# Lag projections in 32-column strips, normalisation on ScalarE, Gram sums per group, and ternary weights loaded and rounded behind the lag chain, in a two-layer kernel

## What is computed

```python
def _L0_xattn_ref(Q, K, V, Wq, bq, Wout, bout):      # K_TOP = 12, 16 heads of 16
    q, k_, v = ((a @ Wq + bq).transpose(0, 2, 1) for a in (Q, K, V))
    corr = real(ifft(fft(q) * conj(fft(k_)))).mean(axis=(0, 1))
    W_topk, I_topk = top_k(corr, K_TOP);  W_topk = softmax(W_topk)
    R = sum(w * roll(v, -shift) for w, shift in zip(W_topk, I_topk))
    return heads_side_by_side(R) @ Wout + bout
...
def _weight_quant(w):
    scale = 1.0 / clip(mean(abs(w)), 1e-05)
    return clip(round(w * scale), -1.0, 1.0) / scale
...
x = x + _L0_xattn_ref(layernorm(x), ctx, ctx, ...)
x = x + top1_of_8_experts(layernorm(x), ...)
x = x + masked_attention_16_heads(layernorm(x), ctx, ctx, mask, ...)
x = x + bitlinear(silu(bitlinear(layernorm(x), w_gate)) * bitlinear(layernorm(x), w_up), w_down)
```

## Time and profile before

| what | value |
|---|---|
| three runs | 1537.13, 1540.78, 1541.70 us (median 1540.78) |
| the profiled execution's own time | 1551.78 us |
| its span | 1550.0 us, mean granted TensorE clock 0.915 |
| busy: PE, weight loads, DVE, ACT, POOL | 1268.1, 878.3, 1097.4, 958.6, 691.8 us |
| mean DMA rate over the span | 140 GB/s |
| the chain that ended last | PE 47%, DVE 22%, issue 14%, ACT 5%, DMA 4% |

### The profile page before, as it was taken

One profiled execution on the slowest core, in us unless ns is written; L12 is line 12 of the kernel. 1 busy time (PEld: TensorE's weight loads), 2 busy tenths in 40 slices (PEclk: granted clock), 3 DMA queues, 4 the chain that ended last, 5 costly groups with the idle time before them and its releaser, 6 DMA issues.

```text
span 1550.0 us, 29933 instructions
## 1 busy us (share of the span) xinstructions
PE 1268.1 (82%) x9486; PEld 878.3 (57%) x9486; DVE 1097.4 (71%) x3076; ACT 958.6 (62%) x1846; POOL 691.8 (45%) x854
## 2 busy tenths in 40 slices
PE   4962365688899989998999899989998999888875
PEld 4851354456566656665666566656665666555543
DVE  4753342458788878887888788878886777777754
ACT  1220231257777767776777777767766777777774
POOL 2312334235544554456445644565446444444331
PEclk9985586699999989998999999999998999999996
DMA  8772354445445445554544455545444444333200
GB/s 273 228 255 56 99 178 146 142 145 157 142 149 155 152 139 150 152 158 134 151 150 150 151 153 148 154 141 150 142 140 127 132 145 126 120 104 103 76 9 14
DMA packets 169174, 216.84 MB, mean 140 GB/s; under 512 B 19002, under 2 KB 157628, under 8 KB 162492
## 3 DMA queue, kind: packets, MB, share of 16 engines
q1 hardware_dynamic: 162876, 198.15, 41.8%
q0 software_dynamic: 6144, 16.79, 3.2%
HBM read 133.33 MB, written 79.43 MB: 137 GB/s over the span
## 4 chain that ended last, share of the span: by engine, by line
PE 47%; DVE 22%; issue 14%; ACT 5%; DMA 4%; POOL 4%; SPq 3%; DVEq 0%; another core or an unknown queue 0%; POOLq 0%; ACTq 0%
DVE mx L1104 8%; PE mx_pair L1369 5%; PE bank L1330 5%; PE ex_pair L1314 4%; PE bank L1442 4%; PE bank L1340 4%; PE bank L1396 3%; PE mx_pair L1292 3%; PE bank L1390 3%; DVE small L1160 3%; PE mx_pair L1356 3%; PE bank L1450 2%; PE bank L1410 2%; DVE t L1155 2%; DVE bn L899 2%
## 5 line engine op out<-in xcount | busy, mean ns | idle before, releaser
L1104 DVE TENSOR_REDUCE mx<-mx_pair 128x4 f32<-128x1024 f32 x256 | 312.7, 1222 | 60.0 <-PE mx_pair L1369 36.2
L694 POOL TENSOR_TENSOR hid<-hid,t 128x256 f32<-128x256 f32 x256 | 196.3, 771 | 227.4 <-DVE t L1155 226.0
L846 ACT ACTIVATE pt<-ex_pair 128x1024 f32<-128x1024 f32 x256 | 262.1, 1024 | 26.0 <-PE ex_pair L1314 25.8
L1369 PE MATMUL mx_pair<-ks,qs 62*128 62x256 f32 x1024 | 133.3, 336 | 67.8 <-DVE mx L1104 57.8
L1330 PE MATMUL bank<-pt,va 128*32 128x256 f32 x2048 | 169.7, 404 | 2.0 <-ACT ot L852 1.9
L1369 PEld LDWEIGHTS mx_pair<-ks,qs 62*128 62x128 f32 x1024 | 85.6, 196 | 144.0 <-DVE mx L1104 120.1
L871 ACT ACTIVATE hid<-bank 128x256 f32<-128x256 f32 x256 | 98.6, 385 | 109.0 <-PE bank L1340 100.3
L1314 PE MATMUL ex_pair<-qs,ks 64*128 64x256 f32 x1024 | 132.5, 338 | 7.8 <-ACT pt L846 7.7
L1442 PE MATMUL bank<-ew,xst 128*128 x480 | 125.5, 406 | 6.4 <-ACT xst L815 6.2
L1155 DVE SCALAR_TENSOR_TENSOR t<-th,bank 128x256 f32<-128x256 f32 x256 | 106.8, 417 | 33.5 <-ACT th L877 21.2
L661 POOL TENSOR_TENSOR rs<-ve,mhalf 128x2 f32<-128x2 f32 x96 | 68.6, 714 | 132.1 <-DVE ve L905 112.0
(11 more groups left out here) (212 smaller groups left out, 2757.4 us busy)
## 6 DMA issues: line engine op xcount, KB each, us to landing
ks<-ksplit_d SPq DMA_DIRECT2D x192, 128.0 KB
qs<-qsplit_d SPq DMA_DIRECT2D x192, 128.0 KB, 3.1
ys_d<-ys SPq DMA_DIRECT2D x56, 256.0 KB, 2.2
xs<-xs_d SPq DMA_DIRECT2D x24, 512.0 KB
x<-in_x SPq DMA_DIRECT2D x32, 256.0 KB, 3.9
va<-in_ctxT SPq DMA_DIRECT2D x32, 256.0 KB, 3.6
xl<-in_x SPq DMA_DIRECT2D x32, 256.0 KB
x_d<-xl SPq DMA_DIRECT2D x32, 256.0 KB, 3.7
```

The costliest lines, as they stand in the source:

```text
L694: pool.tensor_tensor(part_, part_, t1[:, c % 2], ALU.mult).then_inc(hid_made, 1)
L846: act.activation(pt[:, slot:slot + 2].rearrange("p i a c -> p (i a c)"), ex_pair[:, :], ACT.Exp).then_inc(ex_made[u % 2], 1)
L1104: dve.tensor_reduce(mx[:, t].rearrange("p (r g j) -> p r g j", r=2, j=2)[:, :, g], mx_pair[:, :].rearrange("p (r j s) -> p r j s", r=2, j= ...
L1369: ins = pe.matmul(shared_bank(job, r)[:, j * S:(j + 1) * S], qs[par][rows, 2 * g + j, t * P:(t + 1) * P], ks[par][rows, 2 * g + j, :], sta ...
```

## The change

Three parts, all in the set-up but for what they hand over to the pipeline's head.

- **The loop.** x has six buffers instead of four. The normalised rows are written by ScalarE (two instructions of 128x256 a batch) from POOL's root and a second POOL product, instead of by VectorE. A product now uses a 32-column window of `z` and writes one of four strips of 32 partitions: batch b's strip is b % 4. The ctx product is made one batch ahead of the x product, so that two products that follow each other go to different strips. Group banks are doubled, and a group's two Gram products are made as soon as it is out.
- **The loads.** The feed-forward weights are loaded behind the read-back of the Gram matrix, `ew` behind the second `load_x` of the pipeline, `eb_r` and the zeroing of the second scratch area behind the fourth, the zeroing of the first behind the circulant. The small weights go between the last eight batches' loads.
- **The rounding.** The absolute sums follow the picking of lags. The nine passes and POOL's filling of three of the stacks stand in the pipeline, behind the first sort and the first scatter.

```diff
 def pipeline_may_start(eng):
-    eng.wait_ge(tern, 12)
+    eng.wait_ge(tern, 3)
...
 # SP, the loop
+    if b >= XA:                       # 6
+        sp.wait_ge(a_xn, b - XA + 1)
+    sp.dma_start(xa_at(b % XA), x[b]).then_inc(xa_ld[b % XA], 16)
...
+    if b >= CA:                       # 4
+        sp.wait_ge(a_k, b - CA + 1)
+    sp.dma_start(ca_at(b % CA), ctxT[b]).then_inc(ca_ld[b % CA], 16)
...
-for b in range(2): early_x(b, b)
+early_x(0)
+sp.dma_start(wq_raw, ...); sp.dma_start(bq0_c, ...)
+early_ctx(0); early_x(1); early_ctx(1); early_x(2)
+sp.dma_start(wout_s, ...)
+for b in range(2, NB):
+    early_ctx(b)
+    if b + 1 < NB: early_x(b + 1)
+    if b >= NB - GROUP: next(rest, None)     # one small weight each
...
 # POOL, the loop
+pool.tensor_tensor(nm[:, i], mneg[:, i], rs[:, i], ALU.mult).then_inc(a_rstd, 1)
...
 # ACT, the loop
+def apply(b):
+    i = b % 3
+    act.wait_ge(a_rstd, b + 1)
+    if b >= 2: act.wait_ge(a_xnT, b - 1)
+    for t in range(T):
+        ins = act.activation(xna[:, b % 2, t], xa_at(b % XA)[:, t], ACT.Identity, bias=nm[:, i, t:t + 1],
+                             scale=rs[:, i, t:t + 1])
+    ins.then_inc(a_xn, 1)
...
+apply(0)
+for b in range(NB):
+    if b + 1 < NB: apply(b + 1)
+    evacuate(b)
+    if b % GROUP == 1 and b > 1: group_out(b // GROUP - 1)
+group_out(NG - 1)
...
 # PE, the loop
-w = z[:, :, P - L0_DH - L0_DH * j:2 * P - L0_DH - L0_DH * j]
+def product(b, banks, k, src):
+    strip, late = b % STRIPS, b % GROUP // STRIPS
+    at = strip * (P // STRIPS)
+    w = z[:, k, P - L0_DH - late * L0_DH:P + L0_DH - late * L0_DH]
+    return pe.matmul(banks[b // GROUP % 2][at:at + P // STRIPS, 0:S], w, src, start=(late == 0 and k == 0),
+                     stop=(late == 1 and k == KT - 1))
...
+    for k in range(KT):
+        q = product(b, q0_banks, k, xta[:, b % 2, k])
+        kp = product(b + 1, k0_banks, k, ca_at((b + 1) % CA)[:, k])
+    q.then_inc(a_q, 1); kp.then_inc(a_k, 1)
...
+products(-1)
+transposes(0)
+for b in range(1, NB):
+    transposes(b)
+    products(b - 1)
+    if b % GROUP == 4 and b > GROUP: gram(b // GROUP - 1)
+products(NB - 1)
+gram(NG - 1).then_inc(lagstep, 1)
...
 # DVE and POOL, the pipeline
+if job == "sort" and b.quad == FOUR - 1:      # behind slots, DVE
+    if b.n == FOUR - 1: ternary()             # the nine passes
...
+if b.n == FOUR - 1 and c == 2 * FOUR - 1:     # behind the scatter, POOL
+    for i in range(2):
+        pool.wait_ge(tern, 10 + i)
+        pool.memset(qs[i][:].bitcast(F32), 1.0).then_inc(stacks_ready, 1)
+    pool.wait_ge(tern, 12)
+    pool.tensor_copy(ks[0][:], ...).then_inc(stacks_ready, 1)
...
 # waits that the moved loads need
+ pool, first scatter of each area: wait_ge((first_ld, late_ld)[b.four], 16 * 2)
+ act, first xn_b: wait_ge(first_ld, 32); wait_ge(late_ld, 32)
+ dve, first expert: wait_ge(late_ld, 32)      pe, first expert: wait_ge(first_ld, 32)
+ pe, first gate_up: wait_ge(tern, 12)
```

More of the change, by code:

```diff
@@ L38 @@
 XN = 5
+XA, CA = 6, 4
+STRIPS = 4
 HALF = P // 2
@@ L490, in _ @@
-            for dst, src, n in ((bv_r, bv, D), (bo_r, bo, D), (rb_r, rb, NE)):
-                sp.dma_start(dst[:], bass.AP(src.tensor, 0, [[0, P], [1, n]])).then_inc(w_ld, 16)
-            sp.dma_start(eb_r[:], bass.AP(eb.tensor, 0, [[0, P], [1, NE * D]])).then_inc(w_ld, 16)
+            rest = weights()
+            for b in range(2, NB):
+                early_ctx(b)
+                if b + 1 < NB:
+                    early_x(b + 1)
+                if b >= NB - GROUP:
+                    next(rest, None)
@@ new lines, in group_out @@
+            def group_out(g):
+                act.wait_ge(a_q, GROUP * (g + 1))
+                act.wait_ge(a_k, GROUP * (g + 1))
+                act.activation(q0t[:, g], q0_banks[g % 2][:, 0:S], ACT.Identity, bias=bq0_c)
+                act.activation(k0t[:, g], k0_banks[g % 2][:, 0:S], ACT.Identity, bias=bq0_c).then_inc(a_grp, 1)
+            apply(0)
+            for b in range(NB):
+                if b + 1 < NB:
+                    apply(b + 1)
+                evacuate(b)
+                if b % GROUP == 1 and b > 1:
+                    group_out(b // GROUP - 1)
@@ L1188, in _, with transposes @@
             pe.wait_ge(z_made, 1)
-            def transposes(b, j, first):
+            def transposes(b):
                 pe.wait_ge(a_xn, b + 1)
-                if not (first and j < 2):
+                if b >= 2:
                     pe.wait_ge(a_xt, b - 1)
@@ L1214, in _ @@
-            transposes(0, 0, True)
-            for b in range(1, GROUP):
-                transposes(b, b, True)
-                products(b - 1, b - 1, (b - 1) // 4 + 1, None)
-            for g in range(1, NG):
-                transposes(GROUP * g, 0, False)
-                products(GROUP * g - 1, GROUP - 1, 2 * g, None)
-                for j in range(1, GROUP):
-                    transposes(GROUP * g + j, j, False)
-                    products(GROUP * g + (j - 1), j - 1, 2 * g + ((j - 1) // 4 + 1), g)
@@ L1224, in _ @@
-            products(NB - 1, GROUP - 1, NB // 4, None)
-            pe.wait_ge(a_grp, NG)
-            for t in range(T):
-                for g in range(NG):
-                    ins = pe.matmul(bank[t][:, 0:S], k0t[:, g, t * P:(t + 1) * P], q0t[:, g], start=(g == 0), stop=(g == NG - 1))
-            ins.then_inc(lagstep, 1)
+            def product(b, banks, k, src):
[4 more added lines that the diff above has]
+                                 stop=(late == 1 and k == KT - 1))
@@ new lines, in gram @@
+            def gram(g):
+                pe.wait_ge(a_grp, g + 1)
+                for t in range(T):
+                    ins = pe.matmul(gram_banks[t][:, 0:S], k0t[:, g, t * P:(t + 1) * P], q0t[:, g], start=(g == 0), stop=(g == NG - 1))
+                return ins
+            products(-1)
[3 more added lines that the diff above has]
+                products(b - 1)
+                if b % GROUP == 4 and b > GROUP:
+                    gram(b // GROUP - 1)
@@ L1256, in _ @@
             ins.then_inc(lagstep, 1)
+            pe.wait_ge(tern, 1)
+            pe.matmul(bank[5][:, 0:3], ones[:], wabs[:], start=True, stop=True).then_inc(wsum, 1)
             pipeline_may_start(pe)
```

259 lines of the change are left out of this document (118 added, 141 removed).

## The result

| | before | changed |
|---|---|---|
| median of 11 runs each, on one chip | 1541.70 us (1537.13 to 1550.29) | 1534.90 us (1529.34 to 1536.62) |
| profiled execution, its span | 1551.78, 1550.0 us | 1532.26, 1530.5 us |
| mean granted TensorE clock | 0.915 | 0.917 |
| busy: PE, weight loads, DVE, ACT, POOL | 1268.1, 878.3, 1097.4, 958.6, 691.8 us | 1245.0, 841.9, 1073.6, 989.9, 703.1 us |
| first load of the pipeline issued | 146.23 us | 116.14 us |

The ratio is 0.9952, 95% interval 0.9935 to 0.9970: faster by 7 us, where 24 were forecast, and outside the range of 1504 to 1529. The last two rows of the table already tell where to look. The pipeline starts 30.1 us earlier, close to the 31.1 of the forecast, but its first result comes only 7.7 us earlier. Between the two, 22.4 us are given back; the prediction had allowed 7.3.

A forecast was written before the change was run, and what follows sets the result against it. Bounds: PE in the batch loop, single steps in the lag chain, POOL in the pipeline's head. -19.0 - 2.5 - 11.1 + 1.5 + 1.5 + 5.5 + 0.3 = -23.8 us gave 1528 from the profile, 1517 from the median; range 1504 to 1529.

The forecast's parts named there:

- loop: end of the last product: Set-up loop over 32 batches: last product ends at 79 us instead of 98, 19.0 us earlier, at 2.0 us a batch.
- Gram sums: Behind the loop's last group: four records instead of sixteen, saving 2.5 us.
- Gram store: SP's queue: with nothing ahead of it, the store lands 11.1 us earlier.
- weights behind the read-back: Lag chain: the lag weights' store and circulant queue behind 3 MB of weights, 1.5 us lost.
- Rival A: Loop: reaches 1.7 us a batch, bound by ScalarE and loads, if x lands in under 3 us; 1508 us, chance 0.20.
- C: Loop: PE stays the bound, at 2.3 to 2.4 us a batch; 1526 to 1529 us, chance 0.13.
- D: Loop: strips do not overlap and clock falls to 1.2 GHz, 4.6 us a batch; 1598 us, chance 0.05.
- 1.5 us lost: Pipeline head: `ew` stands ahead of stash 0, for which load 2 waits; ends 0 and 5.3, taken as 1.5 us.
- 0, upper end 3: Pipeline head: `eb_r` and second zeroing delay stash 2 and load 4, covered by POOL's wait for the sort; 0 us.
- hidden, but for 0.3 us: Pipeline head: nine passes, 10.8 us, lie in VectorE's idle time beside POOL's first scatter; 0.3 us lost.
- rival B: Pipeline head: scatter and passes exclude each other and run one after the other, 10 us more; 1527 us, chance 0.12.
- the fills, +5.5: Pipeline head: POOL's three fills between first scatter and x2 of batch 5 are not hidden, 5.5 us lost.

The follow-up runs named there:

- y2: The changed kernel with six ctx buffers instead of four, three set-up semaphores merged to make room; median 1524.4 us, ratio 0.9872.
- y1: The changed kernel with the strips undone, every product full width on all 128 partitions; median 1542.3 us, ratio 0.9997.
- y3: The kernel before with zeroing of both scratch areas and `eb_r` moved behind the circulant's load; median 1536.9 us, ratio 0.9956.
- z2: z1 with POOL's three fills put one each behind the roots of batches 1, 2 and 3; median 1530.1 us, ratio 0.9835.
- z3: z2 with the second zeroing ahead of the Gram store and `ew` behind the circulant's load; median 1523.6 us, ratio 0.9812.
- x3: The changed kernel with `ew`, `eb_r` and the second zeroing issued behind the load of batch 5; median 1541.8 us, ratio 0.9909.
- c1: The control: the changed kernel, unaltered, run and profiled again; median 1535.2 us, ratio 0.9964.
- x1: The changed kernel with the nine passes moved from behind the first sort to ahead of the pipeline; median 1536.1 us, ratio 0.9881.
- x2: x1 with POOL's three fills moved from behind the first scatter to behind the root of batch 3; median 1535.7 us, ratio 0.9894.
- z1: The changed kernel with three passes in VectorE's wait for v's product, six beside the attention's store, ones-product ahead of v's product; median 1540.5 us, ratio 0.9899.
- x4: The changed kernel with the edits of x2 and x3 together; median 1532.9 us, ratio 0.9860.
- z4: z3 with the six ctx buffers of y2; median 1516.9 us, ratio 0.9759.

## Why the prediction was wrong, step by step

**Right: everything up to the start of the pipeline.** Predicted gains and what the traces show:

| term | predicted | measured |
|---|---|---|
| loop: end of the last product | 98 to 79 us | 98 to 81.5 us |
| batch 0's products end, and the pace from there | 17 us, 2.0 a batch | 19.4 us, 2.0 a batch |
| Gram sums | -2.5 | -2.5 (last product to Gram store 5.9, now 3.4) |
| Gram store | -11.1 | -11.2 (14.1 from copy to landing, now 2.9) |
| weights behind the read-back | +1.5 | +0.5 (0.8 in the control) |
| first load of the pipeline | near 115 us | 116.1, in the control 118.7 |

The reasons held as well. The pace of 2.0 us comes from the four ctx buffers (y2 has six and gains 9.8 us), the strips overlap (y1), and the queue alone is worth 10.6 of the 11.1 us at the circulant's load (y3). The 2.5 us by which the loop ends late lie at its start: batch 0's products end 2.4 us later than assumed, with transposes and products there at the lower clock (four transposes 1.11 us, later 0.66). Rival A did not happen: x took 3.5 to 7.1 us to land in the chain, not under 3. That y2 gains 9.8 us, where 9 had been worked out for A, is another cause with a like price. Rivals C and D fell: PE's clock is 1.00 in the windows of the loop, and the strips overlap.

**Wrong, first step: "1.5 us lost" for `ew` and "0, upper end 3" for `eb_r` and the zeroing.** The moved loads cost 5.0 us up to the first expert group (z2 to z3; 5.8 from the changed kernel to x3). I subtracted the time that had passed since `ew` was issued, as if `ew` alone stood ahead of the stash and one batch alone were hit. The rows show otherwise: stash 0 takes 7.64 us in the chain, stash 2 occupies the queue for 5.81, and with two buffers every stash stands between a batch and the load of the next but one. The 6.39 us for which the scatter waited for the sort were no cover. On VectorE the statistics of batch 4 stand ahead of batch 3's routing and of the sort, so a late x2 of batch 4 makes the sort late by the same:

```profile
154.24 0.75 DVE L931 BATCH_NORM_STATS2 bn<-xl 128x6 f32<-128x256 f32 x2 [10.55 <-POOL xl L682]
```

The first scatter starts 8.0 us behind that x2 in every profile where x2 came this late (changed, c1, x1, x2, y1, y2, z1, z2). POOL's two waits, for batch 4's rows and for the sort, grew from 1.80 + 6.39 to 11.65 + 4.42 us.

**Wrong, second step: "hidden, but for 0.3 us" for the nine passes; rival B was true.** Scatter and passes do exclude each other: 8.42 us for one instruction, the scatter 17.9 us instead of 10.1 (c1, x3, y1 and y2 show the same; in x1, x2, x4 and z1 to z4, without passes beside it, none is over 1.24). Taking the passes out brings the first expert group 8.8 us forward (z1), so B's price of 10 us was near. It was the half microsecond at 388 us that misled me, and I misread it. I looked at whether the scatter got longer, and it was the pass that did. The same pass, beside nothing of POOL:

```profile
349.39 0.43 DVE L1148 TENSOR_SCALAR xq<-on 128x512 bf16<-128x512 f32 x1 [2.18 <-ACT on L860]
```

Of its 32 instances in the kernel before, 26 take 0.43 us, and the six that start inside a scatter instruction take 0.55 to 0.57. The one at 388.37 is one of these six. So the trace of before already showed the two waiting for each other, with VectorE as the one that came second. With the nine passes back to back it is POOL that waits, until the last one. The Trainium skill, "SBUF — State Buffer", section "SBUF: two separate sides", says that VectorE operations in a mode that takes the port pair shared with GpSimd hold it for the whole instruction, and that the descriptors of a GpSimd DMA are not written meanwhile. The trace agrees: the scatter's second instruction ends 0.8 us after the last of nine passes. That it is the ports, and not something else that the two engines share, no run here separates.

**Nearly right, third step: the fills, +5.5.** They cost 6.4 us up to the first expert group (z1 to z2) and 7.1 in the other pair (x1 to x2).

**What the sum left out: the clock of the groups behind.** At the first expert group the three make 8.8 + 6.4 + 5.0 = 20.2 us, against a loss of 19.4 between before and changed, z3 being 0.9 better there than the kernel before. The prediction had 7.3; of the 12 us that it lacks, the passes are 8.5 and the loads 3.5. Further down come the slow groups: 2.4 us more up to the second scatter, 22.4 in all at the first store. They also blur each single step, which is 3.5, 10.0 and 8.7 us at the second scatter and 2.5, 8.0 and 14.1 at the first store. How the sum divides at the first expert group depends a little on the order too (5.8 for the loads alone in x3, 2.3 in x4).

**What was missing from the method:** I priced each moved load by its own bytes at one place. The head of this pipeline is a chain of trips load, x2, stash, load with two buffers, and whatever lengthens one of them is paid each time.

## What to carry to other kernels

A large transfer is cheap only in a stretch where no small one waits for another: 3 MB behind the Gram read-back cost 0.5 to 0.8 us, 5 MB between the stashes of a double-buffered head cost 5 to 6 us up to the first expert group. When work is moved into "the wait of an engine", ask what the engine beside it does in that wait and whether the two can run together; passes of VectorE and scatters of POOL should not share a stretch here. Before a short overlap in a trace is taken as proof of independence, compare both instructions with their siblings that overlap nothing: 0.55 us against 0.43 would have told. And after a gain at one mark, compare marks further down (here the first expert group, the second scatter and the first store) before believing it: 27 to 30 us at the start were 4 to 8 at the first result.

## What the runs showed of the hardware

- A scatter (indirect DMA issued by POOL) of 0.96 us takes 8.42 us beside fp32 passes of 128x2048 on VectorE, to the hundredth the same in five profiles (changed, c1, x3, y1, y2), and ends behind the last one. An addition of 128x512 on POOL takes 4.6 to 5.0 us beside them instead of 1.26 (x1, x2, x4). The other way round, a VectorE pass of 0.43 us takes 0.55 to 0.57 when it starts inside a scatter instruction (six of 32 in the kernel before).
- The same instructions take different times by the granted clock, and which of them are hit changes from profile to profile. A group of eight expert products is 1.99 us at 2.4 GHz and 3.8 at 1.2 GHz; the changed kernel has two slow ones in its head, y1, with the same head, four. Behind the second scatter all these kernels do the same work up to the first store, yet it takes from 172.7 us (y3, mean clock 0.83, PE busy 128.1) to 179.7 (x3, 0.81, PE busy 132.4); x2 and z2 have 177 to 178 us at 0.80 and 0.79. These 7 us are as large as the whole effect of the change; how much of them is the clock's was not separated. The same kernel, profiled twice, had v's product once at each level, and its start 2.6 us apart.
- Products on two strips that write different banks start within 0.01 us of each other and take 0.22 us per pair, half of what a pair of full-width products takes (0.43, y1).
- The time of one kernel, the one before, differed by 12 us between chips (1542 and 1554). The control met a chip of the first kind, so whether the changed kernel differs as much stays open.
